# Projections and attention in one block of a windowed-attention and mixed-FFN kernel; first stacks loaded from ScalarE's queue, first scores inside the last projection chunk, residual loads at four steps

## The reference, cut to what matters

```python
x = x + _layernorm(attn(_layernorm(x), w_qkv))
x = x + _layernorm(ffn(_layernorm(x), ...))

# attn: 16 heads of 32 features, windows of 128 tokens
qkv = x @ w_qkv                      # 512 -> 1536
scores = einsum('bhnqe,bhnke->bhnqk', q * scale, k_ctx)   # k_ctx: window n-1, n, n+1
out = einsum('bhnqk,bhnke->bhnqe', softmax(scores), v_ctx)

# ffn: per batch of 1024 tokens a mixture of weights from a gate
g  = mean over tokens of (relu(x @ gate_w1.T + gate_b1) @ gate_w2.T + gate_b2)
mW1 = W1 + sum_e g_e TW1_e ;  mW2 = W2 + sum_e g_e TW2_e
out = gelu(x @ mW1.T + mb1) @ mW2.T + mb2
```

## Time and profile before

| | |
|---|---|
| median of 3 runs | 3067.05 us (3061.14 to 3072.29) |
| the profiled execution's own time | 3063.27 us |
| its span in the profile | 3061.4 us |
| busy share of TensorE, VectorE, ScalarE, GpSimd | 95%, 65%, 56%, 27% |
| TensorE granted clock, mean | 0.974 |

### The profile page before, as it was taken

How to read it: one execution, slowest core, us unless ns; L and a number is a source line. 1 busy time by engine, 2 the same in 40 slices (tenths; PEclk the granted TensorE clock), 3 DMA queues, 4 the chain that set the end, 5 groups by cost and what they waited for, 6 DMA issues and landing times.

```text
span 3061.4 us, 55740 instructions
## 1 busy us (share of the span) xinstructions
PE 2909.5 (95%) x20444; PEld 2426.6 (79%) x20444; DVE 1982.6 (65%) x3750; ACT 1726.5 (56%) x3383; POOL 833.9 (27%) x696
## 2 busy tenths in 40 slices
PE   7999999789999999959889999999999999999998
PEld 6888888578888888847777888878887888878886
DVE  4333333278878888857756776786668766776764
ACT  2222222167766666645544666766667666676665
POOL 0000000178888888853310000220004000040003
PEclk9999999899999999979998999999999999999999
DMA  5555554668878788759999776895569766796732
GB/s 192 181 176 169 190 196 165 167 161 198 196 181 193 188 192 196 182 180 354 350 363 355 252 241 204 317 360 206 204 216 384 256 215 227 256 369 213 246 133 83
DMA packets 388931, 697.07 MB, mean 228 GB/s; under 512 B 27192, under 2 KB 159288, under 8 KB 388680
## 3 DMA queue, kind: packets, MB, share of 16 engines
q1 hardware_dynamic: 371648, 652.44, 66.9%
q10 hardware_dynamic: 12960, 25.69, 2.3%
q0 software_dynamic: 4080, 15.73, 1.3%
HBM read 525.45 MB, written 167.78 MB: 226 GB/s over the span
## 4 chain that ended last, share of the span: by engine, by line
PE 44%; DMA 5%; DVE 3%; ACT 2%; SPq 1%; issue 1%; POOL 1%; POOLq 0%; DVEq 0%; ACTq 0%
PE e_hid L1243 7%; PE e_hid L1244 7%; PE e_hid L1245 7%; PE e_acc L1260 7%; PE e_acc L1262 7%; PE e_acc L1261 7%; DMA yl_scratch<-e_yt_lo 4%; DVE e_yt_lo L1504 1%; DMA e_x<-x_scratch 1%; DVE e_c_stats L1477 1%; DVE e_c_y L1498 0%; SPq L1000 0%; ACT e_sums L1375 0%; ACT e_yt_hi L1322 0%; PE e_hid L1224 0%
## 5 line engine op out<-in xcount | busy, mean ns | idle before, releaser
L1554 DVE SCALAR_TENSOR_TENSOR e_part<-e_ring,e_g_cols,e_part 128x512 f32<-128x512 f32 x896 | 622.6, 751 | 2.1
L666 DVE TENSOR_REDUCE b_neg_max<-b_ps_score 128x1 f32<-128x384 f32 (+1 forms) x1024 | 491.4, 526 | 72.6 <-PE b_ps_score L531 61.2
L637 ACT ACTIVATE b_probs<-b_ps_keys 128x384 f32<-128x384 f32 (+1 forms) x1024 | 426.6, 478 | 84.0 <-PE b_ps_keys L546 55.9
L1358 ACT ACTIVATE e_u<-e_hid,e_mb 128x512 f32<-128x512 f32 x256 | 177.3, 693 | 446.2 <-PE e_hid L1245 440.2
L1578 DVE TENSOR_TENSOR e_u_lo<-e_u,e_u_hi 128x512 fp32r<-128x512 f32 x256 | 188.2, 735 | 329.9 <-ACT e_u_hi L1362 329.8
L1133 POOL TENSOR_SCALAR e_var<-e_moments 128x4 f32<-128x4 f32 x15 | 7.8, 523 | 1291.3 <-DVE e_moments L1590 1290.5
L531 PE MATMUL b_ps_score<-b_k_st,b_q_st 96*128 96x384 f32 (+1 forms) x1024 | 334.4, 366 | 15.9 <-DMA b_q_st<-qk_scratch 15.7
L491 POOL TENSOR_TENSOR b_total<-b_probs 128x512 f32<-128x512 f32 x256 | 323.8, 1281 | 69.8 <-ACT b_probs L637 69.7
L546 PE MATMUL b_ps_keys<-b_q_st,b_k_st 97*128 97x384 f32 (+1 forms) x1024 | 314.6, 350 | 27.3 <-DMA b_q_st<-b_max_rows 26.2
L237 DVE TENSOR_TENSOR a_qk<-a_acc,a_qk 128x512 fp32r<-128x512 f32 x128 | 88.5, 691 | 346.1 <-ACT a_qk L176 346.1
L501 POOL TENSOR_TENSOR b_total<-b_total,b_probs 128x512 f32<-128x512 f32 x224 | 286.2, 1278 | 65.7 <-ACT b_probs L637 63.3
(11 more groups left out here) (148 smaller groups left out, 6527.2 us busy)
## 6 DMA issues: line engine op xcount, KB each, us to landing
e_ring<-mix_rows SPq DMA_DIRECT2D x558, 512.0 KB, 5.3
qk_scratch<-a_qk SPq DMA_DIRECT2D x128, 512.0 KB, 2.8
b_k_st<-qk_scratch SPq DMA_DIRECT2D x192, 256.0 KB, 4.3
b_q_st<-qk_scratch SPq DMA_DIRECT2D x192, 256.0 KB, 4.2
a_x_in<-x SPq DMA_DIRECT2D x16, 1024.0 KB, 7.2
v_scratch<-a_v SPq DMA_DIRECT2D x64, 256.0 KB, 3.1
b_v_sb<-v_scratch SPq DMA_DIRECT2D x64, 256.0 KB, 4.9
o_scratch<-b_out SPq DMA_DIRECT2D x128, 128.0 KB, 3.0
```

The costliest lines, as they stand in the source:

```text
L637: act.activation(probs[:, m % RING, h, 0:(hi - lo) * WIN], ps_keys[x % BANKS][:, 0:(hi - lo) * WIN], ACT.Exp, scale=SCALE).then_inc(exp_do ...
L666: dve.tensor_reduce(neg_max[:, g % 2, i, h:h + 1], ps_score[y % BANKS][:, 0:(hi - lo) * WIN], AX_X, ALU.max, negate=True).then_inc(reduced, 1)
L1554: dve.scalar_tensor_tensor(out=part[:, n % 2, half, :], in0=ring[:, slot, :], scalar=g_cols[:, b, e:e + 1], in1=so_far, op0=ALU.mult, op1= ...
```

## The change

1. `phase_qkv` and `phase_attention` become one function and one block, `phase_qkv_attention`; all tiles of both are now called `a_...`. PSUM has eight banks: one score bank and the bank for turns now exist from the start, so the projections keep four accumulators instead of six (`BANKS = 4`). `a_xn` has one buffer instead of two, and VectorE waits for its turns before it writes it again.
2. The 24 loads of the first round's stacks are issued by ScalarE, three behind each of the eight query-key groups of the last chunk but one. ScalarE's exponential table is loaded between the last two chunks.
3. In the last chunk TensorE makes two of the 24 leading scores behind each group and turns the maxima of steps 0 and 1; VectorE reduces them there. SyncE sends the rows of steps 0 and 1 from there. The attention loop now starts at T = 0.
4. The loads of `a_v_sb` follow the last chunk's value stores in SyncE's order, without a wait for those stores to land.
5. `next_x1` is called at `last[run] + 4` instead of `+ 6`.
6. Semaphores that nobody waited for are gone (`table_ready`), and `end_ready` is replaced by `stats_done`.

```diff
@@ constants
-    BANKS = 6
+    BANKS = 4
+    FRONT = AHEAD * UNITS // GROUPS
@@ sync
-                chunk(PAIRS - 1, 0, more=False)
-                chunk(PAIRS - 1, 1, more=False)
-                for s in range(SLOTS):
-                    sp.wait_ge(qk_stored[s], 16 * (1 + CHUNKS * QKG // SLOTS))
-                for p in range(2):
-                    sp.wait_ge(v_stored[p], 16 * QUADS * (1 + PAIRS))
...
-                for c in range(4):
-                    load_k(0, c)
-                    load_q(0, c)
-                for c in range(4):
-                    load_v(0, c)
-                for T in STEPS:
+                chunk(PAIRS - 1, 0, more=False)
+                for g in range(QKG):
+                    store_qk(PAIRS - 1, 1, g)
+                    if g == 5:
+                        row(0)
+                row(1)
+                store_v(PAIRS - 1, 1)
+                sp.wait_ge(v_done, TILES * (CHUNKS + 1))
+                for p in range(2):
+                    sp.wait_ge(v_stored[p], 16 * QUADS * 3)
+                for c in range(4):
+                    load_v(0, c)
+                for T in range(STEPS + LAG):
@@ scalar
                     for g in range(QKG):
                         qk_group(i, p, g)
+                        if prefetch:
+                            (load_k, load_q)[g % 2](act, 0, g // 2)
                         if g >= QKG - KD and not last:
                             xt_block(c + 1, 1 - p, g - (QKG - KD))
...
-                chunk(PAIRS - 1, 0)
+                chunk(PAIRS - 1, 0, prefetch=True)
+                act.activation(unused[:, :], eps[:, :], ACT.Exp)
                 chunk(PAIRS - 1, 1, last=True)
@@ vector
+                    dve.wait_ge(turned, KD * (c + 1))
...
+                for g in range(GROUPS):
+                    for y in range(FRONT * g, FRONT * (g + 1)):
+                        reduce(y // UNITS, y % UNITS)
+                    if g < QKG:
+                        qk_group(CHUNKS - 1, g)
+                    if g == 5:
+                        copy_rows(0)
+                    if g == 9:
+                        copy_rows(1)
@@ tensor
+                for g in range(GROUPS):
+                    group(CHUNKS - 1, 1, g)
+                    for y in range(FRONT * g, FRONT * (g + 1)):
+                        score(y // UNITS, y % UNITS)
+                    if g == 5:
+                        turn_max(0)
+                    if g == 9:
+                        turn_max(1)
@@ phase_gate_ffn
-                        if s == last[run] + 6 and closes(run) and closed_before(run) + 2 < len(closing):
+                        if s == last[run] + 4 and closes(run) and closed_before(run) + 2 < len(closing):
                             next_x1(closed_before(run))
```

More of the change, by code:

```diff
@@ L77, in phase_qkv @@
+        probs = sb("probs", [P, PROBS, QH, 3 * WIN], F32)
+        v_sb = sb("v_sb", [P, W, QH * E], F32)
+        total = sb("total", [P, 2, 2, QH, WIN], F32)
+        out_t = sb("out_t", [P, 2, 3, WIN], F32)
+        out = sb("out", [P, 2, 2, QH * E], F32)
+        ps_score += [psum(f"ps_score{i}", [P, 512]) for i in range(1, TRIO)]
+        ps_keys = [psum(f"ps_keys{i}", [P, 512]) for i in range(TRIO)]
+        ps_out = psum("ps_out", [P, 3, WIN])
         w_loaded = [sem(f"w_loaded{k}") for k in range(KD)]
@@ L248, in chunk, with reduce @@
                         qk_group(c, g)
-                        if g >= QKG - KD and not last:
+                        if g >= QKG - KD:
                             xt_block(c + 1, 1 - p, g - (QKG - KD))
+                def reduce(g, s):
+                    i, h = divmod(s, QH)
+                    lo, hi = span((2 * g + i) % W)
+                    y = UNITS * g + s
+                    if s == 0 and g >= 2:
+                        dve.wait_ge(max_turned, g - 1)
+                    dve.wait_ge(scored, y + 1)
+                    dve.tensor_reduce(neg_max[:, g % 2, i, h:h + 1], ps_score[y % TRIO][:, 0:(hi - lo) * WIN],
+                                      AX_X, ALU.max, negate=True).then_inc(reduced, 1)
@@ L262, in _ @@
                 chunk(PAIRS - 1, 0)
-                chunk(PAIRS - 1, 1, last=True)
+                for g in range(GROUPS):
[7 more added lines that the diff above has]
+                        copy_rows(1)
+                for T in range(STEPS + LAG):
+                    if there(T + AHEAD):
+                        for s in range(3):
+                            reduce(T + AHEAD, s)
+                    if there(T + AHEAD - 1):
+                        copy_rows(T + AHEAD - 1)
+                    if there(T + AHEAD):
+                        for s in range(3, UNITS):
+                            reduce(T + AHEAD, s)
+                    if there(T - LAG):
+                        normalise(T - LAG)
             @block.tensor
@@ L308, in group, with chunk @@
                     product(acc[g % BANKS][:, :], terms).then_inc(acc_done, 1)
-                def chunk(i, p, last=False):
+                def chunk(i, p):
                     c = 2 * i + p
@@ L313, in chunk @@
                         group(c, p, g)
-                        if QKG - KD <= g < QKG and not last:
+                        if QKG - KD <= g < QKG:
                             turn_block(c + 1, 1 - p, g - (QKG - KD))
-                for k in range(KD):
-                    turn_block(0, 0, k)
-                pe.wait_ge(w_lo_done, KD)
-                with pe.Fori(0, PAIRS - 1) as i:
-                    chunk(i, 0)
-                    chunk(i, 1)
-                chunk(PAIRS - 1, 0)
-                chunk(PAIRS - 1, 1, last=True)
```

521 lines of the change are left out of this document (244 added, 277 removed).

## The result

The changed kernel takes 3021.2 us (median of 4 runs, 3013.61 to 3024.29), the kernel before 3064.1 beside it (4 runs, 3056.56 to 3072.29): ratio 0.9864, 95% interval 0.9843 to 0.9885, faster by 1.4%. Forecast were 3012, in a range of 3003 to 3027. The profiled execution, the slowest of the four, took 3024.29 with a span of 3022.5, 38.9 less than the span of before; the medians are 42.9 apart.

The account below looks back on a forecast made before the run. TensorE was taken as the bound, so only its standstills and half clock could be won: 33.0 at the handover plus 19.3 at batch ends, 52.3 off 3063.27, gives 3011.0 (3014.8 from the median); stated 3012, range 3003 to 3027.

Parts of the forecast that it names:

- a rival whose wait of 7 us didn't come: Handover: value loads block, step 2's row comes 4 later, half clock follows; 8 less won, 3020; chance 0.17.
- Work in the last chunk: Handover: 24 scores, two turns and group changes add 5.0 us to TensorE's path; VectorE's maxima stay hidden.
- Moved loads, banks, `a_xn`: Last two projection chunks: ScalarE's stack loads, four accumulator banks and the single buffer cost nothing.
- The rival with ScalarE's queue full: Last chunk but one: blocked load issues push ScalarE's copies by 10 us; some 10 to 15 less, 3025; chance 0.05.
- Steps 0 and 1, head of step 2: Start of attention: VectorE bounds two steps at 8.8; with last scores and lead to step 2's values product, 10.5 us.
- The new wait: Handover: TensorE waits 3.6 us for step 2's row, queued behind value stores and loads; 4 more or nothing as bounds.
- The rival that the row overtakes: Handover: step 2's small transfers pass the loads on free engines, removing the 3.6 wait; 3008; chance 0.08.
- A wait of this length needn't drop the clock: Handover: a wait of 3.6 may leave TensorE at full clock, as one of about 3 did before.
- The signs: Trace marks of being right: first values product at 18 to 19, row wait 3 to 4, `e_x` waits within 1 us, steps of 5.44.
- The residual loads: First three feed-forward batch ends: earlier loads remove GpSimd's 12.02 wait and its late root; 19.3 us won.
- the 0.6 said to stay lost: Batch ends: ScalarE's mixed-weight copy still waits for VectorE, so about 0.6 us remains lost.
- the ring is hit: Batch ends: earlier residual loads delay ring transfers, mixing and ScalarE by up to 2.6 at each of three; 3026; chance 0.06.

Follow-up runs that it names:

- c1: Changed kernel with step 2's row issued ahead of the four value loads and non-urgent mixed-weight copies one step later from step 96: 3008.5 us, ratio 0.9816.
- b2: Changed kernel with step 2's row issued ahead of the four value loads and non-urgent mixed-weight copies one step later from step 24: 3009.9 us, ratio 0.9833.
- b1: Changed kernel with GpSimd's residual additions cut to 4 of 512 columns, loads kept, output different: 3002.7 us (two runs), ratio 0.9809.
- after: The changed kernel itself, measured against the kernel before: 3021.2 us, ratio 0.9864.
- b0: The changed kernel run once more, unaltered, as a measure for later runs: 3017.4 us, ratio 0.9856 to the kernel before.
- a3: Changed kernel with mixed-weight copies not needed within two steps made one step later throughout, on ScalarE and VectorE: 3018.4 us, ratio 0.9862.
- b3: Changed kernel with mixed-weight copies not needed within two steps made one step later, from step 24 only: 3019.1 us, ratio 0.9850.
- a4: Changed kernel with only the row of step 2 issued ahead of the four value loads: 3011.3 us, ratio 0.9830.
- d1: Changed kernel with step 2's row before the value loads, step 3's row behind two, and non-urgent weight copies later from step 96: 3005.0 us, ratio 0.9812.

## Why the prediction was right, and where it was off

The range held the time; the narrower 3006 to 3018, which the forecast itself gave 0.60, did not: 3021.2 lies above it, beside the 3020 of a rival whose wait of 7 us didn't come. The mechanism was right at the handover. In the residual's part the waits went as said, but what runs beside the mixing afterwards was left out. Of the 52.3 forecast, 39.0 came in the profiled execution: 30.5 at the handover, 9.6 at the ends, and 1.1 lost elsewhere.

- **Work in the last chunk**: forecast 5.0, measured 4.7. VectorE's maxima were hidden as said.
- **Moved loads, banks, `a_xn`**: forecast nothing, measured nothing. The rival with ScalarE's queue full is out: the longest three issues took 2.77 together, and its copies kept TensorE going through a stretch in which the DMA engines were full. Three of the 24 issues took more than the 1 us that was to be a sign of being wrong (the longest 1.66), at no cost.
- **Steps 0 and 1, head of step 2**: forecast 10.5, measured 11.2 (6.7 from 582.19 to the beginning of the wait at 588.92, and 4.5 from 594.14 to 598.60). The second part was forecast at 3.5; it ran at half clock.
- **The new wait**: forecast 3.6 with bounds 0 and 7.6, measured 5.2. The row's two DMAs were forecast to be out 6.7 behind the last projection and to land 3.9 later. Their issue began at 6.4 and was over at 7.6 (588.60 and 1.20 for the first two of the four, less 582.19), and TensorE went on at 11.95, that is 4.3 later. So the issuing was 0.9 too short, the landing 0.4, and TensorE came to the wait 0.3 sooner: together the 1.6 that are missing. The rival that the row overtakes is out, and so is the one with a wait of 7; of the latter the half clock came, with the shorter wait.
- **"A wait of this length needn't drop the clock"**: it did here, and it had been priced at nothing. All eight profiles with a wait of 4.3 to 5.2 for the row of step 2 have a clock of 0.52 to 0.66 in 590 to 600; in c1 a wait of 3.0 for the next row was followed by 0.68, while b2's of 2.3 left it at 1.00.
- **The signs**: the first values product was to come 18 to 19 behind the last projection matmul. The prediction's own terms give 10.5 + 3.6 = 14.1; the 5.0 of work in the last chunk lie ahead of that matmul and were counted again. It came at 16.4. The wait was 5.2 instead of 3 to 4, half clock came, GpSimd waited 2.9 for the residual at the first end, and the steps of 5.44 held through the first end only. So two parts of the forecast showed in the trace that they had gone wrong, though the time lay in the range.
- **The residual loads**: forecast 19.3, measured 9.6. That is the step that failed, and three quarters of what was missing (9.7 of 13.3). The waits went as said, and the prediction named rightly what is late next: the copy of mixed weights. But it took over that copy's time from a stretch in which GpSimd stood still. With the residual there in time, GpSimd adds while VectorE mixes, each slow instruction costs 1.04, and the 0.6 said to stay lost (taken off the sum once, as 0.7, though it stands at two ends) became 5.5 and 4.8. The first end lost nothing: there the trace has slow mixing instructions too (four), but no wait of ScalarE for VectorE's mixing; that they fitted into slack is argued, not tested.
- **The rival "the ring is hit"** had the mixing late, as came, but by its transfers. b1 rules these out: with all loads in place and the additions all but gone, the loss is gone.

What stays open: why ends two and three of one kernel differ by up to 1.6 between two profiles (after and b0), what puts the half clock behind some waits of 3 and not behind others (a3 and b3 have the same wait of 3.27), and how much of the differences of 3 to 10 between the medians of the last kernels is theirs, since the attention, which none of them changes, moves a single profile by more. Whether the additions could be kept apart from the mixing altogether was not tried.

## What to carry to other kernels

An engine that waits is also an engine that disturbs nobody. Before a wait is taken away, look at what will run beside what once it is gone, and take the durations of the neighbour from a stretch where both are busy. And when a small transfer that releases the critical engine is late, look at what stands ahead of it in the queue, and having moved it, look at the next of its kind: here TensorE then waited for the second row, in one execution long enough to take back what the first had given, until that row was moved too.

## What the runs showed of the hardware

- A VectorE instruction on two SBUF tiles of 128x512 (float32) takes 0.74 alone and 1.78 beside a GpSimd addition, which itself goes from 1.3 to 1.74. Side by side both come at a common pace of 1.71.
- A row of two transfers of 2 KB, issued behind transfers of 1 MB, let TensorE go on 5.5 to 8.1 us behind the start of its issue (after, a4, b2, c1); behind half of that, and with the stack loads behind it 1.1 later, soon enough that TensorE didn't wait (d1).
- The clock granted after a short wait differs: 1.00 behind 2.3 us (b2), 0.68 behind 3.0 (c1), both in the same place of nearly the same kernel; and behind the same wait of 3.27 in the same place 1.00 (a3) and 0.56 (b3). Over the attention, 650 to 1550, the mean clock lies between 0.95 and 0.97 from profile to profile; c1's profile has 0.95 there and a span of 3022.3, where its median time is 3008.5.
